# Three of sixteen delta*u*B products on GpSimd instead of two, at slots 4, 10 and 15

## What is computed

```
dA  = exp(delta[..., None] * A)                  # decay, 512 channels x 16 states
dBu = delta[..., None] * Bm[:, :, None, :] * u[..., None]
h   = dA_t * h + dBu_t                           # over 1024 time steps
y   = sum over the 16 states of h * C_t
y   = (y + u * D) * silu(z);  out = y @ out_proj_w
```

## Time and profile before

| what | us |
|---|---|
| median of 3 runs | 3021.85 |
| the profiled execution | 3027.0 |
| its span | 3025.2 |
| scan stage within the span | 670 to 2459 |
| DVE busy in the span | 2569.9 |
| POOL busy in the span | 2276.9 |

### The profile page before, as it was taken

The page is one execution under the profiler, slowest core; times in us unless marked ns, Lnnn a source line. Parts: engine busy times, 40 slices in busy tenths (PEclk is TensorE's granted clock), DMA queues, the critical chain, the costliest instruction groups (busy, mean ns, idle before and its releaser), DMA issues. The chain is left out here.

```text
span 3025.2 us, 31486 instructions
## 1 busy us (share of the span) xinstructions
PE 2607.9 (86%) x10147; PEld 1368.9 (45%) x10147; DVE 2569.9 (85%) x2435; ACT 1756.1 (58%) x2337; POOL 2276.9 (75%) x1348
## 2 busy tenths in 40 slices
PE   4999999967878878878878879879877669999998
PEld 2666657633424424424425425425422126666665
DVE  7888875539999999999999999999999967777775
ACT  3554444447766766766767766767765434444442
POOL 4766664249989989989989899899899855655652
PEclk9999999978979979979979979979967679999999
DMA  3111111038898898888988988988988940011000
GB/s 112 32 53 42 53 49 35 24 101 213 196 220 204 204 220 198 209 213 200 213 215 200 218 212 198 214 207 208 217 197 203 233 97 28 29 35 35 28 29 21
DMA packets 183588, 424.67 MB, mean 140 GB/s; under 512 B 23952, under 2 KB 91472, under 8 KB 183184
## 3 DMA queue, kind: packets, MB, share of 16 engines
q1 hardware_dynamic: 164544, 402.19, 54.1%
q10 hardware_dynamic: 18896, 20.65, 2.4%
HBM read 341.88 MB, written 55.71 MB: 131 GB/s over the span
## 5 line engine op out<-in xcount | busy, mean ns | idle before, releaser
L1475 POOL TENSOR_TENSOR mix_scan<-mix_scan,mix_bc 128x1024 f32<-128x1024 f32 x512 | 1199.3, 2358 | 180.3 <-DVE mix_scan L1572 180.0
L1572 DVE TENSOR_TENSOR_SCAN mix_scan<-mix_decay,ps_all 128x1024 f32<-128x1024 f32 x512 | 1166.5, 2284 | 71.4 <-ACT ps_all L1516 24.4
L885 PE MATMUL ps_all<-ffn_w_gate_up,ffn_xT 128*128 128x512 f32 (+1 forms) x1536 | 654.0, 562 | 13.7 <-DVE ffn_h L612 9.4
L1525 ACT ACTIVATE mix_decay<-mix_decay,mix_a_neg 128x1024 f32<-128x1024 f32 x512 | 575.0, 1142 | 105.1 <-DMA mix_decay<-delta_rows 103.6
L1626 PE MATMUL ps_all<-mix_stack,mix_sel 96*128 96x512 bf16 x896 | 317.6, 442 | 322.5 <-DVE mix_scan L1572 309.2
L1582 DVE TENSOR_TENSOR ps_all<-ps_all,mix_bc 128x1024 f32<-128x1024 f32 x448 | 541.0, 1208 | 20.6 <-PE ps_all L1626 20.5
L885 PEld LDWEIGHTS ps_all<-ffn_w_gate_up,ffn_xT 128*128 128x128 f32 x1536 | 278.6, 192 | 245.9 <-issue 201.1
L758 POOL TENSOR_TENSOR ffn_h_scaled<-ffn_h,ffn_h_recip 128x1408 f32<-128x1408 f32 x64 | 168.6, 2635 | 243.6 <-ACT ffn_h_recip L853 243.6
L1608 PE MATMUL ps_all<-mix_scan,mix_red 128*32 128x512 f32 x2048 | 336.2, 738 | 7.7 <-POOL mix_scan L1475 7.7
L612 DVE TENSOR_TENSOR ffn_h<-ffn_silu_gate,ps_all 128x704 f32<-128x704 f32 x128 | 113.6, 887 | 269.6 <-ACT ffn_silu_gate L800 266.0
L1626 PEld LDWEIGHTS ps_all<-mix_stack,mix_sel 96*128 96x128 bf16 x896 | 69.1, 102 | 599.4 <-DVE mix_scan L1572 409.9
(11 more groups left out here) (132 smaller groups left out, 3835.5 us busy)
## 6 DMA issues: line engine op xcount, KB each, us to landing
mix_decay<-delta_rows SPq DMA_DIRECT2D x512, 512.0 KB, 9.6
mix_dbu_aside<-delta_u_rows SPq DMA_DIRECT2D x64, 512.0 KB, 10.7
mix_stack<-mix_parts SPq DMA_DIRECT2D x384, 64.0 KB, 2.5
delta_rows<-mix_delta SPq DMA_DIRECT2D x32, 512.0 KB, 3.1
ffn_x<-_attn_hidden_states_dram SPq DMA_DIRECT2D x32, 256.0 KB, 2.9
after_ffn<-ffn_y SPq DMA_DIRECT2D x32, 256.0 KB, 3.0
normed_ffn<-ffn_y_normed SPq DMA_DIRECT2D x32, 256.0 KB, 3.1
mix_x_tokens<-normed_ffn SPq DMA_DIRECT2D x32, 256.0 KB, 12.8
```

The lines of the kernel that those rows point to most:

```text
L885: ins = M(psG[:, lo:hi], xT[:, j % 2, (t * KX + k) * P:(t * KX + k + 1) * P], wgu[:, k, lo:hi], start=(k == 0), stop=(k == KX - 1))
L1475: G.tensor_tensor(wt, wt, bc[r % 2][:, 1, :], ALU.mult).then_inc(hc_done, 1)
L1525: A.activation(da[:, at % SPREADS, :], da[:, at % SPREADS, :], ACT.Exp, scale=const.aneg[:, qi:qi + 1]).then_inc(exp_done, 1)
L1572: V.tensor_tensor_scan(w[:, slot % RING, :], da[:, slot % SPREADS, :], ps_du[:, slot % 2, :], 0.0, ALU.mult, ALU.add).then_inc(scan_done, 1)
```

## The change

GpSimd makes the product for slots 4, 10 and 15 of each chunk. The DRAM buffer for delta*u holds three groups of 8 rows, filled by three stores of 8 rows in place of one of 24 rows. `spread_du` goes five slots ahead (was seven), POOL's product three slots ahead (was four) but ahead of that slot's hc (was behind it), which is the same place between two hc. The counts follow.

```diff
--- before.py
+++ after.py
@@ -999,8 +999,16 @@
 QUAD = 6
 
 
-EVERY, ASIDE_IN, ASIDE = 8, 7, 4
-ASIDE_FROM = 104
+
+ASIDE_AT = (4, 10, 15)
+ASIDE_IN, ASIDE = 5, 3
+
+
+def slot_row(s):
+
+    return 32 * (s % 4) + 8 * (s // 4)
+
+
 
 
 def round_jobs(r, n_batches, full):
@@ -1070,7 +1078,7 @@
 
     delta_dram = nc.dram_tensor("delta_rows", [2, DI, L], F32, kind="Internal").ap()
 
-    du_dram = nc.dram_tensor("delta_u_rows", [2, CHUNKS, P - ASIDE_FROM, L], F32, kind="Internal").ap()
+    du_dram = nc.dram_tensor("delta_u_rows", [2, CHUNKS, len(ASIDE_AT), NCH, L], F32, kind="Internal").ap()
 
     S = a.sem
     du_kept, aside_in, aside_done, aside_put = S("du_kept"), S("aside_in"), S("aside_dbu_done"), S("aside_put")
@@ -1117,14 +1125,18 @@
                 for m, (s, k, rel, n) in enumerate(mine)]
 
     def is_aside(slot):
-        return slot % EVERY == EVERY - 1
+        return slot % SLOTS in ASIDE_AT
+
+    def asides(slot):
+        c, s = divmod(slot, SLOTS)
+        return c * len(ASIDE_AT) + sum(at <= s for at in ASIDE_AT)
 
     def nth_aside(R, slot):
-        return R * (64 // EVERY) + (slot + 1) // EVERY
+        return R * CHUNKS * len(ASIDE_AT) + asides(slot)
 
     def nth_vector(R, slot):
 
-        return R * (64 - 64 // EVERY) + (slot + 1) - (slot + 1) // EVERY
+        return R * (64 - CHUNKS * len(ASIDE_AT)) + (slot + 1) - asides(slot)
 
     def nth(kind, b, n):
 
@@ -1166,7 +1178,8 @@
 
     def keep_du(sy, b, par, c):
         sy.wait_ge(du_done, chunk(b, c))
-        sy.dma_start(du_dram[par, c, :, :], du[ASIDE_FROM:P, :]).then_inc(du_kept, 16)
+        for n, s in enumerate(ASIDE_AT):
+            sy.dma_start(du_dram[par, c, n, :, :], du[slot_row(s):slot_row(s) + NCH, :]).then_inc(du_kept, 16)
 
     def log_delta(act, n):
         act.wait_ge(taken["D"], n * 2)
@@ -1191,7 +1204,7 @@
 
     def leave1(pool, n):
         pool.wait_ge(cast1, n)
-        pool.wait_ge(du_kept, 16 * n)
+        pool.wait_ge(du_kept, 16 * len(ASIDE_AT) * n)
         nc.gpsimd.tensor_tensor(du[:, :], du[:, :], parts[:, 0, :], ALU.subtract).then_inc(rest1, 1)
 
     def part2(act, n):
@@ -1421,13 +1434,12 @@
 
             def spread_du(r, R, slot):
                 c, s = divmod(slot, SLOTS)
-                if s == EVERY - 1:
-                    sy.wait_ge(du_kept, 16 * chunk(R, c))
-                if slot >= EVERY or r > 0:
+                if s == ASIDE_AT[0]:
+                    sy.wait_ge(du_kept, 16 * len(ASIDE_AT) * chunk(R, c))
+                if slot > ASIDE_AT[0] or r > 0:
                     sy.wait_ge(aside_put, nth_aside(R, slot) - 1)
-                row = 32 * (s % 4) + 8 * (s // 4) - ASIDE_FROM
                 sy.dma_start(aside[:, :],
-                             du_dram[r % 2, c, row:row + NCH, :].unsqueeze(0).to_broadcast([NST, NCH, L]))\
+                             du_dram[r % 2, c, ASIDE_AT.index(s), :, :].unsqueeze(0).to_broadcast([NST, NCH, L]))\
                   .then_inc(aside_in, 16)
 
             def program(r, R, full):
@@ -1469,15 +1481,15 @@
             def program(r, R, full):
                 for slot in slots(r):
                     c, s = divmod(slot, SLOTS)
-                    if core(r, full):
-                        pool.wait_ge(scan_done, R * 64 + (slot + 1))
-                        wt = w[:, slot % RING, :]
-                        G.tensor_tensor(wt, wt, bc[r % 2][:, 1, :], ALU.mult).then_inc(hc_done, 1)
                     rr, R2, at = ahead(r, R, slot, ASIDE)
                     if core(rr, full) and is_aside(at):
                         pool.wait_ge(aside_in, 16 * nth_aside(R2, at))
                         G.tensor_tensor(aside[:, :], aside[:, :], bc[rr % 2][:, 0, :], ALU.mult)\
                          .then_inc(aside_done, 1)
+                    if core(r, full):
+                        pool.wait_ge(scan_done, R * 64 + (slot + 1))
+                        wt = w[:, slot % RING, :]
+                        G.tensor_tensor(wt, wt, bc[r % 2][:, 1, :], ALU.mult).then_inc(hc_done, 1)
                     b, cc = (R, c + 1) if c < 3 else (R + 1, 0)
                     par = (r if c < 3 else r + 1) % 2
                     if (c < 3 and core(r, full)) or (c == 3 and -1 < r < B - 1):
```

## The result

The changed kernel takes 3119.56 us (median of 4 runs, 3116.45 to 3120.68) against 3021.47 us: ratio 1.0318, interval 1.0306 to 1.0331. It is slower by 98 us, as forecast in sign and inside the range of 3040 to 3130 us; the forecast was 3085 us. The profiled execution took 3119.3 us, its span 3117.5 us.

What follows compares the result with a forecast made beforehand. DVE sets the pace now; POOL was to become the bound, with 1685 us of work, 155 us of waits and 12 us idle: stage 1852 against 1789 us. 3027 + 63 - 5 = 3085 us, range 3040 to 3130.

Steps and rivals of the forecast that it cites:

- The wait for the spread of slot 15: Spread behind SP's third restack: POOL waits 5.1 us in 24 chunks and 4.7 us in 7, together 155 us.
- POOL becomes the bound: Scan stage: POOL's 1685 us of work plus 155 us of waits make 1840 us; with 12 us idle, stage 1852 us.
- under 40 was asked: Sign in the changed profile: POOL's wait for scans falls from 180 us to under 40 us.
- the 80 asked for: Sign in the changed profile: DVE waits 80 us or more for the put L1528.
- some 31: Sign in the changed profile: POOL's product L1487 has some 31 waits for the aside DMA, 100 to 210 us.
- The margins for slots 10 and 4, costed at nothing: POOL's spreads for slots 10 and 4 land in time, with margins of 1.7 and 0.2 us; cost taken as nothing.
- the 5 us taken off for the median: The sum uses the profiled execution of 3027.0 us; the runs' median is 5 us lower, subtracted at the end.
- Neither end is on the path: nothing: ACT gains 32 copies of 1.02 us, PE loses 32 replications; neither is on the path, so no cost.
- the faster rival: DVE stays the bound: slot 15's spread lands in time, stage 1747 us, time 2980 us; chance 0.08.
- the slower one's clause on the put of slot 10: Three-waits rival: put late behind ACT's cast waiting for REST1, or margins gone; 2 us more a chunk, 3147 us; chance 0.06.
- The port rival: Shared SBUF port: each product moved to POOL stops DVE for 2.31 us instead of 1.30, +32 us, 3054 us; chance 0.02.
- Loads and slack: POOL's 180 us of waits for scans are its only slack; added products and waits, 229 us, are more.

Runs made afterwards that it cites:

- e1: Changed kernel with all its spreads of delta*u issued seven slots ahead in place of five: 3056.7 us, ratio 1.0101 to the kernel before.
- e7: Changed kernel with the spread for slot 15 alone issued seven slots ahead, those for 4 and 10 still five: 3064.0 us, ratio 1.0144 to the kernel before.
- e2: Changed kernel with all its spreads issued six slots ahead in place of five: 3072.8 us, ratio 1.0163 to the kernel before.
- e3: Kernel before (two products aside, slots 7 and 15) with only its spreads five slots ahead in place of seven: 3077.0 us, ratio 1.0178.
- e4: Changed kernel with the three products at slots 3, 9 and 15 and spreads seven slots ahead: 3017.2 us, ratio 0.9982 to the kernel before.
- e5: Changed kernel with the three products at slots 3, 8 and 13, spreads still five slots ahead: 3065.9 us, ratio 1.0150 to the kernel before.

## Why the prediction was right, and by how much it was off

*The wait for the spread of slot 15.* Right in place, cause and size: 155 us forecast, 160 measured, and the times within a chunk agree to 0.1 us. e1 and e7 take it away by issuing the spread earlier, and e2 shows that its place behind the restack decides.

*POOL becomes the bound.* Right as a sum: scans leave it idle for only 25 us (under 40 was asked). Its added products are in the stage too: busy 1679 us, 1685 forecast. DVE's 135 us for puts are above the 80 asked for. Its busy time is 1673 us where 1666 was forecast, and 48 of POOL's products wait for the tile, not some 31.

*The margins for slots 10 and 4, costed at nothing.* This is the term that was mis-sized in the sum. The waits for the tile are 183 us, not 155: 5 us more at slot 15 and 24 us at slots 4 and 10, of which 6 us each stand at the start of the stage and in the last chunk, which the forecast had not looked at. The whole sum then reads 1679 us of work, 183 us for the tile and some 14 us for scans within the stage, which is 1876 of the 1879 us measured; 6 us less work than forecast hide some of the 28 us. The stage is so 27 us over the forecast. The rest of the 35 us missed is mainly the 5 us taken off for the median, which the changed kernel's profiled execution does not stand above, and some 1 us outside the stage.

*"Neither end is on the path: nothing", for ACT.* Wrong, and hidden in the changed kernel by the larger wait. ACT's load shows no cost of its own, but its order does: the puts of slots 4 and 10 stand behind the logarithm and the second cast. Without any wait for the tile the change still loses 34 us of stage (e1): DVE's own 1747 us, 58 us more of waits for puts (82 against 24, with what ends as "issue" at slot 4), 13 more for PE, and some 4 us that are not in these terms. So the faster rival's 2980 us could not have come about with these slots, and the slower one's clause on the put of slot 10 was the better guess. The port rival falls: DVE's scans and POOL's products last as long as before in all kernels (2286 and 2356 ns in the changed one), and DVE's idle time ahead of scans in gaps of under 0.15 us is 37 us before and after.

*Loads and slack.* I took the wait to matter because POOL had become full. e3 shows it costs 46 us of stage with POOL not full, through the put. The two costs apart, 46 (e3) and 34 us (e1), add up to 80 of the 91 us of the changed kernel; the 11 us left may come of having both, when POOL has no slack left to win back what a chunk has lost. No run isolates that.

## What to carry to other kernels

Before moving work to an engine that looks less busy, write down, for each hand-over that the work adds, what stands just ahead of it in the row of every engine and queue that passes it on; here SP's restack and ACT's logarithm and cast decided the time, not the 74 us of work that POOL took on, as e4 shows with the same work. A spread issued by slot numbers is only as early as the last wait ahead of it in the issuing queue (e2, e5). The same three products, two of them one slot earlier and all spreads two slots earlier, turn +3.2% into -0.2%, which is to be read as no change.

## What the runs showed that was not expected

The gain that remains is small where DVE's loads promise much more: e4 takes 42 us of products off DVE and returns 3 to 5 us of time (10 us of stage in the profiled executions), since waits for puts (+21 us), for the decay, and for PE ahead of products and the gate take the rest. And the time that a spread of 512 KB takes to land goes with what was issued just ahead of it: 6.5 us for slot 15 in the changed kernel, behind one spread of delta, and 11 to 15 us for slot 3 in e5, behind four or five.
